# A tiled Perceiver block: the key bias of the context attention moved from TensorE to VectorE, and its output products one step later

## The reference

```python
def _L1_xattn_ref(image_emb, text_emb, edge_index, Wq, bq, Wk, bk, Wv, bv):
    scale = D ** (-0.5)
    q = jnp.einsum('bsd,ed->bse', image_emb, Wq) + bq
    k = jnp.einsum('bsd,ed->bse', text_emb, Wk) + bk
    v = jnp.einsum('bsd,ed->bse', text_emb, Wv) + bv
    scores = jnp.einsum('bqd,bkd->bqk', q, k) * scale
    probs = jax.nn.softmax(scores, axis=-1)
    attended = jnp.einsum('bqk,bkd->bqd', probs, v)
    return attended
...
x = x + _L0_ffn_ref(_layernorm(x, axis=-1), L0_ffn_w_gate, L0_ffn_w_up, L0_ffn_w_down)
x = x + _L1_xattn_ref(_layernorm(x, axis=-1), ctx_1024, L1_xattn_edge_index, ...)
x = x + _L1_attn_ref(_layernorm(x, axis=-1), ...)
```

## Time and profile before

| | |
|---|---|
| time, median of 3 runs | 753.7 us (753.58 to 753.89) |
| span of the profiled execution | 751.1 us, some 2.6 us below the runs' times |
| TensorE busy | 662.8 us (88%) |
| VectorE busy | 485.5 us (65%) |
| ScalarE busy | 365.0 us (49%) |
| GpSimd busy | 310.1 us (41%) |
| chain that ended last | PE 64%, DVE 21%, ACT 5% |

### The profile page before, as it was taken

How to read it: one execution, slowest core, us unless ns; L and a number is a source line. 1 busy time by engine, 2 the same in 40 slices (tenths; PEclk the granted TensorE clock), 3 DMA queues, 4 the chain that set the end, 5 groups by cost and what they waited for, 6 DMA issues and landing times.

```text
span 751.1 us, 16917 instructions
## 1 busy us (share of the span) xinstructions
PE 662.8 (88%) x6115; PEld 500.4 (67%) x6115; DVE 485.5 (65%) x1367; ACT 365.0 (49%) x992; POOL 310.1 (41%) x458
## 2 busy tenths in 40 slices
PE   4899999999999989985994799988999776999990
PEld 3677878787777778753443586667877673777760
DVE  2686777677768669885488873558888875333330
ACT  1454545545555479874395653436566431222320
POOL 1235455646453179850000031136556513556541
PEclk9999999999999999996997699999999986999995
DMA  8723222322220000019200434538001022243434
GB/s 265 245 62 79 64 78 65 78 65 75 68 72 14 1 3 4 3 44 332 103 0 1 156 125 177 217 125 367 2 3 65 3 99 53 47 69 58 68 40 70
DMA packets 31697, 65.08 MB, mean 87 GB/s; under 512 B 5792, under 2 KB 21792, under 8 KB 29312
## 3 DMA queue, kind: packets, MB, share of 16 engines
q1 hardware_dynamic: 26016, 55.73, 22.8%
q0 software_dynamic: 4688, 7.18, 6.0%
q10 hardware_dynamic: 912, 1.10, 0.5%
HBM read 57.67 MB, written 7.37 MB: 87 GB/s over the span
## 4 chain that ended last, share of the span: by engine, by line
PE 64%; DVE 21%; ACT 5%; issue 4%; DMA 2%; SPq 2%; POOL 1%; DVEq 0%; ACTq 0%; POOLq 0%
PE psum L2627 7%; PE psum L474 6%; PE psum L482 6%; PE psum L496 5%; PE psum L2637 4%; PE psum L521 4%; PE psum L507 4%; PE psum L1482 3%; PE psum L1459 3%; PE psum L837 2%; DVE ff_peak L1500 2%; PE psum L846 2%; PE psum L829 2%; PE psum L877 2%; DMA wn<-in_w_down 2%
## 5 line engine op out<-in xcount | busy, mean ns | idle before, releaser
L415 ACT ACTIVATE prob<-s_sb,negm 128x257 f32<-128x257 f32 x128 | 66.2, 517 | 94.5 <-DVE negm L640 94.5
L782 POOL TENSOR_SCALAR bias<-dist,cst 128x257 f32<-128x257 f32 x128 | 59.8, 486 | 99.5 <-DVE dist L627 89.6
L636 DVE CUSTOM_DVE_ANT_0 s_sb<-psum,bias 128x257 f32<-128x257 f32 x128 | 49.4, 423 | 51.7 <-PE psum L496 48.4
L474 PE MATMUL psum<-ctxT,shared 128*128 128x257 f32 x256 | 62.6, 388 | 2.7 <-DMA msk<-in_mask 2.7
L482 PE MATMUL psum<-shared,ctxT 128*128 128x256 f32 x256 | 60.4, 379 | 0.0
L2627 PE MATMUL psum<-ex_w,shared 128*128 x184 | 58.3, 460 | 0.6 <-ACT shared L2520 0.6
L1721 POOL TENSOR_TENSOR wn<-wn,cst 128x1 f32<-128x1 f32 x8 | 4.7, 589 | 120.4 <-DVE wn L1848 120.4
L474 PEld LDWEIGHTS psum<-ctxT,shared 128*128 128x128 f32 x256 | 47.2, 195 | 9.0 <-issue 3.4
L482 PEld LDWEIGHTS psum<-shared,ctxT 128*128 128x128 f32 x256 | 48.4, 189 | 6.8
L496 PE MATMUL psum<-kT,qbd 64*128 64x257 f32 x256 | 48.4, 429 | 3.0 <-DVE mx L636 2.9
L2627 PEld LDWEIGHTS psum<-ex_w,shared 128*128 128x128 f32 x184 | 33.1, 190 | 15.4 <-issue 0.8
(11 more groups left out here) (359 smaller groups left out, 1655.9 us busy)
## 6 DMA issues: line engine op xcount, KB each, us to landing
ctxT<-in_ctx_T SPq DMA_DIRECT2D x32, 257.0 KB
ex_w<-in_w SPq DMA_DIRECT2D x1, 5632.0 KB, 17.5
kpos<-in_kpos SPq DMA_DIRECT2D x32, 128.5 KB
msk<-in_mask SPq DMA_DIRECT2D x32, 128.5 KB
near_turned<-in_ctx_T_tiles SPq DMA_DIRECT2D x4, 1028.0 KB
ff_used_up<-in_ctx_T_tiles SPq DMA_DIRECT2D x4, 1028.0 KB
near_rows<-in_ctx_tiles SPq DMA_DIRECT2D x4, 1024.0 KB, 8.0
ff_used_up<-in_ctx_tiles SPq DMA_DIRECT2D x4, 1024.0 KB, 7.3
```

The costliest lines, as they stand in the source:

```text
L415: nc.scalar.activation(prob[n % 2][:, g, :], s_sb[n % 2][:, g, :], ACT.Exp, bias=negm[:, b, g:g + 1], accum_out=esum[t % 2][:, b, g:g + 1]) \
L474: ins = nc.tensor.matmul(kv[m][:, 0:SK], w["xa_k"][:, k, P * m:P * m + P], ctxT[n % BT][:, k, :], start=(k == 0), stop=(k == KT - 1))
L636: nc.vector.tensor_tensor_reduce(s_sb[n % 2][:, g, :], sc[g % 2][:, 0:SK], bias[n % 2][:, g, :], 1.0, float("-inf"), ALU.add, ALU.max, mx[ ...
L782: nc.gpsimd.tensor_scalar(bias[n % 2][:, g, :], dist[n % 2][:], c.slope[:, g:g + 1], 1.0, ALU.mult, ALU.mult).then_inc(bias_ready, 1)
```

## The change

Three things. The number qb is now made by VectorE: it multiplies the normalised tile with key_row, a row of 256 numbers that stands in all partitions, and sums along the row, right behind the normalising in `norm_apply`, and adds the offset. The two one-column products on TensorE and ScalarE's L1757 go; key_row is made once from two more products of 256 columns and one copy of 128x256. Second, the output product, its add, and with them the reciprocal's buffer, come one step later (tile u - 2 in step u), which needs a step NT + 1 at the end, behind the segment attention's pieces. Third, the order in a step changes: on TensorE the output product comes first, the token products move behind the two turns, and scores and weighted context are adjacent; on ScalarE the exponential comes first and the copy of the projected token last.

```diff
@@ the loops of the block: TensorE, VectorE
         segment.pe(pe, -1)
+        context.pe(pe, NT + 1)
         pe.wait_ge(context.y_done, NT)
...
         segment.dve(dve, -1)
+        context.dve(dve, NT + 1)
@@ act_step
+            if there(u):
+                act.wait_ge(nb_ready, u + 1)
+                at_least(act, mix_ready, u - 1)
+                nc.scalar.activation(prob[u % 2][:], s_bank[:, 0:SK], ACT.Exp, bias=nb[u % 2][:], scale=SCALE,
+                                     accum_out=esum[u % 2][:]).then_inc(e_ready, 1)
             if there(u + 3):
...
-                nc.scalar.activation(qb[n % 2][:], k_bank[:, D:D + 1], ACT.Identity, bias=offset[:], scale=SCALE) \
-                    .then_inc(k_done, 1)
@@ pe_step
+            if there(u - 2):
+                n = u - 2
+                pe.wait_ge(m_done, n + 1)
+                at_least(pe, y_done, n)
+                project_tokens(nc, y_bank, mixT, w["cx_v"]).then_inc(y_full, 1)
             if there(u + 3):
...
-                for k in range(KT):
-                    ins = nc.tensor.matmul(k_bank[:, D:D + 1], xT[n % 2][:, k, :], key_bias[:, k:k + 1],
-                                           start=False, stop=True, skip_group_check=True)
-                ins.then_inc(k_full, 1)
...
-            if there(u - 1):
-                n = u - 1
-                pe.wait_ge(m_done, n + 1)
-                at_least(pe, y_done, n)
-                project_tokens(nc, y_bank, mixT, w["cx_v"]).then_inc(y_full, 1)
@@ norm_apply
             nc.vector.tensor_scalar(xn[i][:], x[:, n, :], mv[i][:, 0:1], rstd[i][:], ALU.subtract, ALU.mult) \
                 .then_inc(xn_ready, 1)
+            dve.wait_ge(xn_ready, n + 1)
+            st.link(dve, nc.vector.scalar_tensor_tensor(
+                bias_wide[:].rearrange("p k t -> p (k t)"), xn[i][:], SCALE, key_row[:], ALU.mult, ALU.mult,
+                accum_out=qb[:, n:n + 1]))
+            st.link(dve, nc.vector.tensor_scalar(qb[:, n:n + 1], qb[:, n:n + 1], offset[:], None, ALU.add))
@@ dve_consts
-            nc.vector.tensor_copy(key_bias[:], y_bank[:, KT:2 * KT])
...
+            nc.vector.tensor_copy(key_row[:], y_bank[:, D:2 * D]).then_inc(consts_done, 1)
+            dve.wait_ge(consts_done, 1)
@@ dve_step
                 dve.wait_ge(s_full, n + 1)
-                dve.wait_ge(k_done, n + 1)
...
-            if there(u - 1):
-                n = u - 1
+            if there(u - 2):
+                n = u - 2
                 dve.wait_ge(y_full, n + 1)
                 dve.wait_ge(bias_added, n + 1)
```

More of the change, by code:

```diff
@@ L1748, in act_step @@
                 nc.scalar.copy(mixT[:], m_bank[:, 0:D].rearrange("p (k t) -> p k t", k=KT)).then_inc(m_done, 1)
+            if there(u):
+                act.wait_ge(p_full, u + 1)
+                at_least(act, a_full, u)
+                nc.scalar.copy(pT[:], p_bank[:, 0:2 * P].rearrange("p (i t) -> p i t", i=2)).then_inc(p_done, 1)
             if there(u + 2):
@@ L1752, in act_step @@
                 at_least(act, s_full, n - 1)
-                at_least(act, nb_ready, n - 1)
                 for m in range(KT):
-                    nc.scalar.activation(qk[n % 2][:, m, :], k_bank[:, P * m:P * m + P], ACT.Identity,
-                                         bias=column[:, m:m + 1])
-                nc.scalar.activation(qb[n % 2][:], k_bank[:, D:D + 1], ACT.Identity, bias=offset[:], scale=SCALE) \
-                    .then_inc(k_done, 1)
[L1759 to L1762, removed]
+                    ins = nc.scalar.activation(qk[n % 2][:, m, :], k_bank[:, P * m:P * m + P], ACT.Identity,
+                                               bias=column[:, m:m + 1])
+                ins.then_inc(k_done, 1)
         def pe_start(pe):
@@ L1773, in pe_start @@
             first = True
-            for i, (left, right) in enumerate(((w["cx_k"], w["cx_bq"]), (w["cx_q"], w["cx_bk"]))):
-                for m in range(KT):
-                    for k in range(KT):
-                        nc.tensor.matmul(y_bank[:, KT * i + m:KT * i + m + 1], left[:, k, P * m:P * m + P],
-                                         right[:, k:k + 1], start=first, stop=True, skip_group_check=True)
-                        first = False
+            for m in range(KT):
+                for k in range(KT):
+                    nc.tensor.matmul(y_bank[:, m:m + 1], w["cx_k"][:, k, P * m:P * m + P], w["cx_bq"][:, k:k + 1],
+                                     start=first, stop=True, skip_group_check=True)
+                    first = False
             for k in range(KT):
-                ins = nc.tensor.matmul(y_bank[:, 2 * KT:2 * KT + 1], bias_wide[:, k, :], w["cx_bk"][:, k:k + 1],
+                nc.tensor.matmul(y_bank[:, KT:KT + 1], bias_wide[:, k, :], w["cx_bq"][:, k:k + 1],
+                                 start=False, stop=True, skip_group_check=True)
+                ins = nc.tensor.matmul(y_bank[:, D:2 * D], bias_wide[:, k, :], w["cx_q"][:, k, :],
                                        start=False, stop=True, skip_group_check=True)
@@ L1791, in pe_step @@
                 turn_tokens(nc, x_bank, xn[n % 2], c).then_inc(xT_full, 1)
[L1792 to L1799, removed]
-                                         skip_group_check=True)
-                for k in range(KT):
-                    ins = nc.tensor.matmul(k_bank[:, D:D + 1], xT[n % 2][:, k, :], key_bias[:, k:k + 1],
-                                           start=False, stop=True, skip_group_check=True)
-                ins.then_inc(k_full, 1)
             if there(u - 1):
@@ L1815, in pe_step @@
                 ins.then_inc(p_full, 1)
+            if there(u + 2):
+                n = u + 2
+                pe.wait_ge(xT_done, n + 1)
+                at_least(pe, k_done, n)
+                for m in range(KT):
+                    for k in range(KT):
+                        ins = nc.tensor.matmul(k_bank[:, P * m:P * m + P], fold[:, k, P * m:P * m + P],
+                                               xT[n % 2][:, k, :], start=(m == 0 and k == 0), stop=True,
+                                               skip_group_check=True)
+                ins.then_inc(k_full, 1)
             if there(u + 1):
```

24 lines of the change are left out of this document (9 added, 15 removed).

## The result

The changed kernel took **758.67 us** (756.62 to 759.64) against 753.64 of the kernel before in the same measurement, a ratio of 1.0072 with a 95% interval of 1.005 to 1.0094: slower. Forecast: 755.0, range 752.0 to 757.3. The profiled run took 756.62 and spans 754.8 us, 3.7 above the 751.1 of before.

A forecast was written before the change was run, and what follows sets the result against it. VectorE was taken to bound the stretch at step 0, TensorE the full context steps. Later FFN tile 1.6, steady steps -3.8, block's end 2.2, clock 1.3 sum to +1.3 us: 755.0, range 752.0 to 757.3.

The forecast's parts named there:

- Price of the new pair: VectorE, FFN loop: product with a sum and small add, with waits, cost 0.80 us a tile, between 0.60 and 1.23.
- The dear rival: VectorE's product with a sum makes the price 1.1 us a tile; five tiles add 1.5, 756.5 us; chance 0.08.
- Maximum, exponential and turn at step 0: First maximum on VectorE at 450.53, 4.0 us later; exponential 0.04 after its chain; TensorE's turn at 452.05, 0.74 later.
- The clock: After TensorE's 3.85 us wait at step 0, a 3.4 us stretch at the lower clock costs 1.3, between 0.8 and 1.7.
- The steady steps: TensorE's context steps until the last weighted context starts: net 3.8 us less, after 0.8 given back for waits.
- The three savings: TensorE's steps: key-bias products gone 1.85 us, fewer tiling switches 1.8, output product of tile 7 moved out 0.97.
- a late mix: TensorE's turn of the mix waits for VectorE's maximum, add and mix; some 0.8 us given back in all.
- The end of the block: TensorE waits for tile 7's add, starting its next piece 2.5 us later; VectorE's reciprocal comes 2.2 later.
- the 0.29 of slack: End of the block: ScalarE's four copies end at 509.80, 0.29 us before VectorE's reciprocal at 510.09.
- The rival of a second fall: The clock falls again in the 2.5 us wait at the block's end, about 1.5 us more, 756.5; chance 0.11.
- The faster rival: Late TensorE at the block's end is absorbed by VectorE's chain, costing 0.5, clock stays high: 752.0 us; chance 0.18.
- The likeliest sign: Whole kernel: slower, above 755.2 us, chance 0.43, against same 0.39 and faster 0.18.

The follow-up runs named there:

- the last step first: The changed kernel with the output product and add of tile 7 ahead of the segment attention's last pieces on TensorE and VectorE; 755.40 us, 1.0008.
- the bias alone: The kernel before with only the key bias moved to VectorE, orders and output products as they were; 751.29 us, 0.9961.
- the bias alone, maximum first: The kernel before with the key bias on VectorE and the first maximum ahead of the statistics of tile 4; 751.50 us, 0.9959.

## Why the prediction was wrong

**Price of the new pair (0.80 a tile): right.** It measured 0.84. The product with its sum lasts 0.42 to 0.43 us, as long as the plain add of the same size that has one input in PSUM (L1630, 0.42), and the read of the sum 0.08 more, most of it overlapped. The dear rival fell: the Trainium skill's rule of halved throughput ("Vector Engine (DVE) Microarchitecture Reference", Points that are easy to get wrong), under which it would be near 0.69, an estimate (0.43 and the 0.26 of the prediction), does not show here.

**Maximum, exponential and turn at step 0: right,** to 0.3 us (0.2 from the price, 0.1 from ahead of the loop), and that VectorE is the cause is shown by the kernel without the product.

**The clock (+1.3): the term that failed first.** I expected one stretch of 3.4 us and cut it to 1.3, since part would fall on the wait. It was 6.8 us, with all of step 0 in it: 2.7 by the kernels whose step 0 has the same order at the full clock (3.17 against 5.88). I had bounded the term at 1.7 from a single row, after a different kind of stretch, and a row is no bound.

**The steady steps (-3.8, measured -2.5): the savings right, the wait that eats them wrong.** The three savings made 4.62 in my sum and 4.82 where nothing takes them back; the bias's part 1.84 for 1.85, the order and the product of tile 7 3.0 for 2.77. I gave back 0.8 for a late mix. What came was a wait for the add of the tile before, 2.3 us in four steps: the output product now opens the step, the add it needs still stands behind the next maximum on VectorE, and both share one bank. The diff shows this wait (`at_least(pe, y_done, n)`); I priced the move by what stood around it on TensorE and didn't ask which wait the moved instruction carried along.

**The end of the block (+2.2): the wait right, its cost not.** VectorE's add ended to 0.01 us when I had said, and the 0.29 of slack was right. But I let TensorE start at once, and it started 0.56 after the add: 3.05 later instead of 2.5. And the clock fell behind the wait too, 1.3 more from L2109 to L904. So the reciprocal was 4.1 late instead of 2.2, counted from the last weighted context. The rival of a second fall had 0.11, though I had given the same effect the most likely case at step 0. The measured sum at the reciprocal is 4.65 - 2.5 + 4.1 = 6.2, where I had 1.3.

**What lies behind.** Of 6.2 late at the reciprocal 3.7 is left at the end of this profile and 5.0 in the median of the runs. That a delay here can shift or remove a low-clock stretch in a later stage was no part of the sum. The faster rival (a late TensorE absorbed) is refuted by the last step first: taking the wait away gave 3.3.

The likeliest sign was right (slower 0.43), though the forecast's 755.0 itself lay just inside of no change. The size was wrong by 4.9 at the reciprocal: 1.4 for the clock at step 0 (2.7 less 1.3), 1.3 for the clock at the block's end, 1.5 for the wait for the add (2.3 less 0.8), 0.6 for TensorE's late start at the end, 0.3 for the turn, less 0.2 of savings. That it is 3.7 in the time is the 1.2 that came back behind, which I had not foreseen either.

**Open.** Why the bias alone gains 0.4% when its rows show 0.9 us, 0.1%, from the FFN loop to 503 us: in its profile two low-clock stretches of before are missing, but one profile of each doesn't tell whether that holds in all runs. Nor is it settled what makes the clock fall: a wait of 2.69 us at step 0 left it alone in both profiles that have it, while one of 2.38 to 2.58 us at the end of the block, with waits of 1.42 and 0.46 close ahead, was followed by the fall in all eight that have it (L837 then lasted 3.25 to 3.76 us). So the length of the wait alone doesn't decide.

## What to carry to other kernels

When an instruction is moved to the front of a step, list the waits it carries (buffer free, not only data ready) and find where each releaser stands on its own engine: here a buffer's release stood behind another tile's maximum, and it cost 2.3 us of the 3.0 that the new order and the late output saved. Work given to an idle-looking engine is charged where that engine leads; put the result that others wait for ahead of the new work, and leave filler work ahead of the wait, not behind it. Where a wait on TensorE grows by a few us, count what follows at the lower clock too, since it can cost nearly as much as the wait: here 2.7 us behind 3.57.

## What I had not expected of the hardware

A little more waiting brought the whole fall of the clock: 2.69 us without work at step 0 left it at 1.00 in two kernels, 3.57 or 3.58 there, in four profiles of three kernels, brought 6.8 us at the lower level, 1.2 GHz. Work of no use put in the wait (2.74 us of products, 1.01 of wait left) kept it up, and the 2.7 us behind the wait came back.

A product with a sum on VectorE (128x256, both inputs in SBUF) lasts no longer than one without: 0.43 us against 428 ns for 128x257, with a read of the sum of 0.08 that starts before the product's end.

A table load that stands directly ahead of a waiting exponential costs nothing (445.44, then 5.02 us of wait), while behind a copy that is itself late it costs its full 1.28 on the path (451.97 to 453.26, the bias alone, maximum first).
